# Loop work at other steps, and the single taps of two images' 3x3 convolution as 64-row matmuls on the two halves of the array

## What is computed

```python
om = conv3x3(x, w_om) + b_om                     # 64 -> 108 channels: o1, o2, mask
o1, o2, mask = split(om, 3)                      # 4 groups x 9 taps each
offset, mask = concat(o1, o2), sigmoid(mask)     # offset: (dy, dx) per tap and group
# for each tap k: v_k = bilinear sample of x at (position + tap k + (dy, dx)) * mask
out = relu(sum_k w_dcn[:, :, k] @ v_k)           # 64 -> 64 channels
```

## Time and the profile before

| | |
|---|---|
| time, median of 3 runs | 207.06 us (206.66 to 207.31) |
| the profiled execution's own time | 207.24 us |
| its span, first to last instruction | 205.1 us |
| busy: PE, DVE, ACT, POOL | 180.4, 161.3, 106.3, 86.2 us |
| mean granted TensorE clock | 0.998 of full speed |

### The profile page before, as it was taken

How to read it: one execution, slowest core, us unless ns; L and a number is a source line. 1 busy time by engine, 2 the same in 40 slices (tenths; PEclk the granted TensorE clock), 3 DMA queues, 4 the chain that set the end, 5 groups by cost and what they waited for, 6 DMA issues and landing times.

```text
span 205.1 us, 4582 instructions
## 1 busy us (share of the span) xinstructions
PE 180.4 (88%) x1806; PEld 127.2 (62%) x1806; DVE 161.3 (79%) x268; ACT 106.3 (52%) x199; POOL 86.2 (42%) x103
## 2 busy tenths in 40 slices
PE   0398997979899989999889999999969999998980
PEld 0234944644356544477578779639958789877870
DVE  0899778994768859887889779717999798899922
ACT  1146057500007784688748757836766687864000
POOL 8237952864013096504444344240661554442000
PEclk9999999999999999999999999999999999999999
DMA  6940000000130000010011000000002000000000
GB/s 189 327 33 2 3 0 0 3 0 0 29 77 19 20 27 9 25 36 3 9 36 25 0 3 0 3 0 3 9 25 70 20 2 16 0 16 2 19 0 21
DMA packets 8499, 5.54 MB, mean 27 GB/s; under 512 B 4887, under 2 KB 7461, under 8 KB 8473
## 3 DMA queue, kind: packets, MB, share of 16 engines
q1 hardware_dynamic: 8089, 4.25, 8.1%
q10 hardware_dynamic: 288, 0.89, 1.4%
q0 software_dynamic: 96, 0.06, 0.1%
HBM read 2.82 MB, written 0.52 MB: 16 GB/s over the span
## 4 chain that ended last, share of the span: by engine, by line
PE 66%; DVE 16%; ACT 6%; issue 4%; DMA 3%; POOL 2%; SPq 0%; DVEq 0%; ACTq 0%; POOLq 0%
PE ps L1254 20%; PE ps L1228 10%; PE ps L1148 10%; PE ps L1044 4%; PE ps L1165 3%; DVE smp_prod L777 3%; DMA x_parts<-in_x 3%; PE ps L1296 3%; PE ps L1302 3%; PE ps L1081 3%; PE ps L1213 2%; PE ps L1199 2%; DVE smp_prod L888 2%; PE ps L1182 2%; DVE windows_attention L873 1%
## 5 line engine op out<-in xcount | busy, mean ns | idle before, releaser
L888 DVE TENSOR_TENSOR smp_prod<-ps,hx_selx 128x768 f32<-128x768 f32 x72 | 67.5, 953 | 10.1 <-PE ps L1228 8.8
L1254 PE MATMUL ps<-smp_prod,windows_attention 128*64 128x192 f32 (+2 forms) x512 | 54.9, 336 | 0.0
L1254 PEld LDWEIGHTS ps<-smp_prod,windows_attention 128*64 128x64 f32 x512 | 40.1, 136 | 4.1 <-ACT windows_attention L575 0.3
L1228 PE MATMUL ps<-haty,by_rows 128*64 128x256 f16 x432 | 39.4, 275 | 2.0 <-DVE smp_prod L888 1.8
L451 POOL TENSOR_SCALAR disty<-disty 64x512 f32<-64x512 f32 (+1 forms) x23 | 13.5, 586 | 64.3 <-ACT haty L596 64.2
L1228 PEld LDWEIGHTS ps<-haty,by_rows 128*64 128x64 f16 x432 | 26.1, 109 | 9.7 <-DVE smp_prod L888 3.9
L604 ACT ACTIVATE hx_selx<-ps 128x512 f32<-128x512 f32 x36 | 21.3, 591 | 10.8 <-PE ps L1213 10.8
L458 POOL TENSOR_TENSOR haty<-disty,haty 64x512 f16<-64x512 f32 (+1 forms) x23 | 24.0, 1042 | 1.9
L1148 PE MATMUL ps<-conv_staged 128*108 128x512 f32 (+1 forms) x60 | 23.3, 521 | 0.7 <-ACT x_parts L568 0.7
L606 ACT ACTIVATE hx_selx<-hx_selx 128x512 f32<-128x512 f32 x36 | 22.7, 631 | 1.2
L591 ACT ACTIVATE disty<-ps 128x512 f32<-128x512 f32 (+1 forms) x24 | 12.5, 521 | 12.3 <-PE ps L1199 12.3
(11 more groups left out here) (140 smaller groups left out, 273.2 us busy)
## 6 DMA issues: line engine op xcount, KB each, us to landing
x_parts<-in_x SPq DMA_DIRECT2D x2, 256.0 KB, 5.2
bcast<-in_bcast SPq DMA_DIRECT2D x2, 256.0 KB, 6.6
x2seq<-x_parts SPq DMA_DIRECT2D x2, 256.0 KB, 3.7
out<-x_parts SPq DMA_DIRECT2D x8, 64.0 KB, 2.2
vals_attw<-in_cf ACTq DMA_DIRECT2D x1, 480.0 KB, 5.8
stack_m<-x_parts SPq DMA_DIRECT2D x12, 36.0 KB
kept<-in_cf ACTq DMA_DIRECT2D x1, 390.5 KB, 4.2
conv_staged<-in_wom SPq DMA_DIRECT2D x1, 324.0 KB, 6.8
```

What stands on the lines that cost most here:

```text
L888: nc.vector.tensor_tensor(pairs, rows, cols.unsqueeze(1).to_broadcast([P, QUARTERS, HW]), ALU.mult).then_inc(s_mult, 1)
L1228: ins = nc.tensor.matmul(ps[h * C:(h + 1) * C, at:at + HW], by_matrix(a, QUARTERS - 1 - k)[:, h * C:(h + 1) * C], haty[i % 2][:, p * HW:(p ...
L1254: return nc.tensor.matmul(dst[:, at:at + strips * 3 * SP].rearrange("p (s k n) -> p s k n", k=3, n=SP), rows, sampled(i, ki, m, first, str ...
```

## The change

Three tables of the loop are new, one more step constant moves, and the single taps are done in another way. The weights' upper half, zeros before, is filled by one POOL copy with the single taps' weights. A single tap is then a matmul on 64 rows only. Pieces 0 and 1 interleave theirs: those of piece 0 read partitions 0 to 63, those of piece 1 partitions 64 to 127, and they write different PSUM banks (4 and 0). In pieces 2 to 4 the single tap is a 64-row matmul between two 128-row ones.

```diff
-MASKS = [{4: (0, 0), 5: (0, 1), 6: (0, 2), 8: (0, 3)}, {0: (0, 4), 2: (0, 5), 6: (1, 0), 8: (1, 1)},
+MASKS = [{4: (0, 0), 5: (0, 1), 7: (0, 2)}, {0: (0, 3), 1: (0, 4), 3: (0, 5), 5: (1, 0), 7: (1, 1)},
...
-    (1, 2): (9, 6), (1, 3): (10, 6), (1, 4): (11, 4), (1, 5): (12, 4),
+    (1, 2): (9, 6), (1, 3): (10, 6), (1, 5): (11, 4), (2, 2): (12, 6), (2, 3): (13, 6), (2, 5): (14, 4),
+    (3, 2): (15, 6), (3, 3): (16, 6)}
...
-SEL_Y = {1: 0, 3: 1, 7: 2}
+SEL_Y = {2: 0, 6: 1, 8: 2}
-LATE = {0: (1, 1), 1: (2, 0), 2: (2, 1)}
+LATE = {0: (1, 1), 2: (2, 0), 3: (2, 1)}
...
+            pool.wait_ge(s_wom, 16)
+            singles = womt.rearrange("p (k s n) -> p k s n", k=3, s=2)[:, :, 1]
+            nc.gpsimd.tensor_copy(singles[C:P], singles[0:C]).then_inc(s_singles, 1)
+            pool.wait_ge(s_singles, 1)
...
-                    if m == 3 and i:
+                    if m == 4 and i:
                         values(i - 1, 2, it)
...
-                        if (i, m - 1) in PAIRS_AT:
-                            g, src = PAIRS_AT[i, m - 1]
-                            if g % 2:
+                        for at in (m - 1, m):
+                            g, src = PAIRS_AT.get((i, at), (0, 0))
+                            if g % 2 and (at == m) == (i > 0 and src == 4):
                                 window_out(g, it, src)
...
+            def conv_single(p, ky, upper, start, stop):
+                n, lo, hi = PIECES[p]
+                rows = slice(C, P) if upper else slice(0, C)
+                return nc.tensor.matmul(bank(CONV_BANK[p])[0:OM, lo:hi], womt[rows, (2 * ky + 1) * OM:(2 * ky + 2) * OM],
+                                        conv_source(PIECES[p], rows, 3 * ky + 2 - upper), start=start, stop=stop,
+                                        skip_group_check=True)
...
-            for p in range(2):
-                for k in range(TAPSTEPS):
-                    convolve(p, k)
+            pe.wait_ge(s_singles, 1)
+            pe.wait_ge(s_dup0, 1)
+            for ky in range(3):
+                conv_pair(0, ky, ky == 0, False)
+            pe.wait_ge(s_dup0, 2)
+            for ky in range(3):
+                ins = conv_single(0, ky, 0, False, ky == 2)
+                conv_single(1, ky, 1, ky == 0, False)
+            ins.then_inc(s_conv, 1)
+            for ky in range(3):
+                ins = conv_pair(1, ky, False, ky == 2)
+            ins.then_inc(s_conv, 1)
```

More of the change, by code:

```diff
@@ L280, in bass_local_attention_then_deformable_conv @@
         s_perm, s_wtap, s_wzero, s_wfin = sem("s_perm"), sem("s_wtap"), sem("s_wzero"), sem("s_wfin")
+        s_singles = sem("s_singles")
         s_stats, s_pair, s_eps, s_rstd = sem("s_stats"), sem("s_pair"), sem("s_eps"), sem("s_rstd")
@@ L1137, in _, with conv_source, conv_pair @@
             keep_warm(3)
+            def conv_source(piece, rows, tap):
+                n, lo, hi = piece
+                j = n % 2 * 2 + lo // HW
+                return shifted(dup[n // 2], tap)[rows, j:j + (hi - lo) // HW]
+            def conv_pair(p, ky, start, stop):
+                n, lo, hi = PIECES[p]
+                return nc.tensor.matmul(bank(CONV_BANK[p])[0:OM, lo:hi], womt[:, 2 * ky * OM:(2 * ky + 1) * OM],
+                                        conv_source(PIECES[p], slice(0, P), 3 * ky), start=start, stop=stop,
+                                        skip_group_check=True)
+            def conv_single(p, ky, upper, start, stop):
+                n, lo, hi = PIECES[p]
+                rows = slice(C, P) if upper else slice(0, C)
+                return nc.tensor.matmul(bank(CONV_BANK[p])[0:OM, lo:hi], womt[rows, (2 * ky + 1) * OM:(2 * ky + 2) * OM],
+                                        conv_source(PIECES[p], rows, 3 * ky + 2 - upper), start=start, stop=stop,
+                                        skip_group_check=True)
             def convolve(p, k):
-                n, lo, hi = PIECES[p]
-                h, j = n // 2, n % 2 * 2 + lo // HW
+                n = PIECES[p][0]
                 ky, single = divmod(k, 2)
                 if k == 0:
-                    if h == 0:
-                        pe.wait_ge(s_dup0, n % 2 * 2 + hi // HW)
+                    if n < 2:
+                        pe.wait_ge(s_dup0, J)
                     else:
                         pe.wait_ge(s_dup1, 2)
-                ins = nc.tensor.matmul(bank(CONV_BANK[p])[0:OM, lo:hi], womt[:, k * OM:(k + 1) * OM],
-                                       shifted(dup[h], 3 * ky + 2 * single)[:, j:j + (hi - lo) // HW], start=(k == 0),
-                                       stop=(k == TAPSTEPS - 1), skip_group_check=True)
+                if single:
+                    ins = conv_single(p, ky, 0, False, k == TAPSTEPS - 1)
+                else:
+                    ins = conv_pair(p, ky, k == 0, False)
                 if k == TAPSTEPS - 1:
@@ L1333, in sampling @@
                         if i < 3 and m == 6 and isinstance(it, int):
-                            windows_out(8 + 4 * i, it)
+                            windows_out(8 + 3 * i, it)
                         if i == 0 and m == 8 and isinstance(it, int):
@@ L1358, in sampling @@
                         g, dst = PAIRS_AT[i, m]
-                        if i == 0 or m in (3, 5):
+                        if i == 0 or m == 3:
                             windows_out(g - 1, it)
@@ L1366, in sampling @@
                     if m == FINAL and i:
-                        if i in (1, 2) and isinstance(it, int):
-                            windows_out(6 + 4 * i, it)
+                        if i in (1, 2, 3) and isinstance(it, int):
+                            windows_out(7 + 3 * i, it)
                         if i == FAR and isinstance(it, int):
@@ L1371, in sampling @@
                         final(i - 1, it)
-                for m in range(3):
+                for m in LATE:
                     block_of_products(B - 1, *LATE[m], it)
```

5 lines of the change are left out of this document (2 added, 3 removed).

## The result

| | before | changed kernel |
|---|---|---|
| time, median of the runs timed side by side | 207.34 us (206.66 to 207.48) | 205.53 us (204.86 to 205.99) |
| the profiled execution's own time | 207.24 us | 205.50 us |
| its span | 205.1 us | 203.6 us |
| mean granted TensorE clock | 0.998 | 0.997 |

The ratio is 0.9916, with a 95% interval of 0.9895 to 0.9937: the changed kernel is 0.6% to 1.1% faster. The forecast was 204.6 us with a range of 202.9 to 207.2; the time lies 0.9 us above the forecast.

What follows compares the result with a forecast made beforehand. The prediction took the loop as bound by PE with DVE close behind. Its terms, 0.0 - 1.5 - 1.5 - 0.2 + 0.45 = -2.75, rounded to -2.6, took the profiled 207.24 to 204.6 us, range 202.9 to 207.2.

Steps and rivals of the forecast that it cites:

- convolution ahead of the loop: Before the loop: first select_y 0.2 us earlier, two splits between the select_y's 0.22 later; net 0.0, ends -0.45 and +0.35.
- windows: In the loop: three PE waits for DVE's copies of window groups, 1.82 us together, mostly go; -1.5 us.
- bank 7 with the late block and its values: Loop: PE's stops for ACT's copy at PSUM bank 7 half won, -1.5 us; block and values one step later, -0.2.
- piece 4: Steps (3, 4) and (3, 5): alternating pairs and single taps make four new splits where PE is the bound, +0.45 us.
- POOL's copy: Copy of the single taps' weights on POOL: hidden in a 4.23 us gap, costs nothing; 0.5 us without that gap.
- the time of the interleaved passes: Sign in the convolution: the interleaved single taps' matmuls take about 1.5 us and not 2.6.
- the windows without a wait: Sign in the loop: no idle time of PE above 0.3 us before windows.
- the stretches: Signs between successive `final`s: 1 and 2 shorter by 1.2 to 1.8 us each, 3 about 1 longer, 5 and 6 0.3 to 0.7 shorter.
- The price of a split: PE going between matmuls on all and part of the array: 0.11 us each, from two convolution runs; a pass 0.437.
- the stops only move: Rival: PE, freed at bank 7, waits for DVE's multiplication instead; only -0.3 us in all, 206.9 us, chance 0.17.
- Row halves one after the other: Rival: the 12 interleaved single-tap passes don't run side by side, 2.62 us instead of 1.53; 205.5 us, chance 0.15.
- The late vertical weights: Rival: the spread in step 1 of images 1, 3, 5, 7 waits 0.85 us each for POOL; 208.0 us, chance 0.18.

Runs made afterwards that it cites:

- conv_only: Kernel before with only the convolution changed to the changed kernel's, 64-row single taps in all pieces; 208.49 us, ratio 1.0047.
- loop_only: Kernel before with the changed kernel's loop tables, values step and window-copy rule, convolution as before; 203.92 us, ratio 0.9821.
- bank7_and_late: Kernel before with the new masks, select_y steps, late block and values step; windows and convolution as before; 204.98 us, ratio 0.9869.
- own_weights: Changed kernel with the copied single-tap weights in their own buffer, so pieces 2 to 4 run single taps on 128 rows; 204.42 us, ratio 0.9839.
- singles_one_half: Changed kernel with piece 1's single taps also on partitions 0 to 63, behind those of piece 0; 205.99 us, ratio 0.9931.
- windows_only: Kernel before with only the windows' steps and the rule for their copies from the changed kernel; 207.48 us, ratio 0.9993.
- bank7_only: Kernel before with only the MASKS and SEL_Y tables of the changed kernel; 211.3 us, ratio 1.0192.
- late_only: Kernel before with only the blocks of steps 1 and 2 and the third values one step later; 207.23 us, ratio 0.9984.

## Why the prediction was right, and where its sizes were off

The sign and the range were right, and the main mechanisms in part. The sizes came out by some luck, as errors of both signs met in the sum. The terms, each beside what the runs showed:

| term of the prediction | predicted | measured | by |
|---|---|---|---|
| convolution ahead of the loop | 0.0 | +0.45 | start of conv_only against before, +0.43, and of the changed kernel against loop_only, +0.47 |
| windows | -1.5 | -0.65 | sums of loop_only and bank7_and_late |
| bank 7 with the late block and its values | -1.5 - 0.2 | -2.2 | sums of bank7_and_late and before |
| piece 4 | +0.45 | +0.7 | stretch 3, conv_only and own_weights |
| POOL's copy | 0 | 0 | start of the convolution, 59.40 in the changed kernel against 59.42 |

The measured terms add up to -1.7; the trace has -1.75. The table leaves out two small parts, the start of loop_only, 0.17 us earlier than before, and the last stretch, 0.05 longer, and it rounds the rest. The prediction's own sum was -2.75, rounded to -2.6.

Of the signs that it named, the time of the interleaved passes and the windows without a wait came. Of the stretches, only stretch 1 fell as said (1.54); 2 gained 0.91 where it said 1.2 to 1.8, 3 lost 1.87 where it said about 1, 6 gained 0.89 where it said 0.3 to 0.7, and 5 got longer. In stretch 3 the term for piece 4 was too small, and two groups of windows moved in: at 0.59 us each they alone are 1.2, so that with 0.45 for piece 4 the sum is 1.6.

**Ahead of the loop.** This term went wrong at "A DMA that took all of the 2.57 us would make the select_y 0.11 later, one that took 1.8 or less gives all of the 0.66. I take -0.2." The DMA takes nearly all of it. The chain of the changed kernel holds the pieces, from DVE's last part to the select_y:

```profile
64.50 0.44 DVE x_parts L862
64.94 0.43 SPq L368
65.38 0.04 issue
65.42 1.87 DMA stack_y<-x_parts
67.28 0.14 issue
67.42 0.30 PE ps L1226 x2
```

From the end of DVE's part to the select_y are 2.48 us, with no slack. If the transfer took as long before the change, the select_y was within 0.1 us of being bound by it then already (2.57 us from DVE's part), though the trace of before showed it right behind PE's own work. PE won 0.52 of the 0.66 us (it was free at 66.81, where it had started the select_y at 67.33), and this could only become a wait, of 0.61 with the 0.09 by which the select_y came later. The two splits had been counted as 0.22; they are 0.33. Both misses have one sign, 0.3 and 0.1 us.

**The price of a split.** This is the step that made piece 4 and the second select_y too cheap: "18x + s = 7.98 and 8x + s = 3.61 give x = 0.437 and s = 0.11". The two runs differ in more than their length, since the first one holds 24 passes of 256 columns, and s is the small remainder of two large numbers: 0.1 us more or less in them moves it by 0.08 or 0.18. The rows to take were two short runs of equal passes, and the chain of the kernel before has both, the 8 passes in 3.61 us of the earlier trace rows and

```profile
136.33 1.90 PE ps L1148 x4
```

They give 0.43 and 0.19, without an edit. With 0.18 piece 4 would have been +0.72 and measured +0.71. The interleaved passes were taken for seven slots; the pairs in own_weights make six, and with one entry, 6 x 0.215 + 0.18, that is the 1.48 us from 60.85 to the next pass on 128 rows at 62.33.

The Trainium skill ("TensorEngine Tiling (Array Packing)", Key Properties) says that a change of tiling mode drains the engine. The runs agree in kind, with 0.16 to 0.18 us a change, and between windows and tap, both on 128 rows and over 64 columns wide, there is no such price: the tap's two passes take 0.86 us in the kernel before, twice 0.43. The page "TensorE: Matmul & The Clock Gate" of the Trainium skill (Packing small matmuls) says in one sentence that weights load under running matmuls only where the row group differs. In another of the same section it also names loads into a background weight buffer. The runs speak against the first sentence alone: in singles_one_half all twelve passes are on one row group and take 2.77 us, 0.23 each, where passes with their loads in the open would need 0.22 and 0.17 more.

**Windows.** "The three waits sum to 1.82; I take -1.5" took waits for time. PE was to go on to the next spread, and that one waits for the multiplication of the step before on DVE. In windows_only this takes all of the gain. In the full set of tables 0.65 us are left; that DVE's work stands more evenly there is a likely reason, not a tested one. The rival "the stops only move" named exactly this wait, before the spreads, but priced it at bank 7; it held for the windows instead.

**Bank 7, block and values.** The term was -1.7 and the runs gave -2.2. The mechanism was right where it was named (the chain no longer goes through ACT in (5, 3)), but the size came in part from elsewhere: stretches 3 to 6, which had the stop and were to give 1.5, gave 1.02 in bank7_and_late (0.08, 0.26, -0.21 and 0.89), stretch 7 gave 0.60 where 0.2 was put down, and stretches 1 and 2 gave 0.57, which no term had. As a sum of two parts the term was wrong: priced one by one they are +4 and 0. The prediction had put the values' step down to evening out PE's work; bank7_only shows that it is what lets the masks move in image 1, and the waits in late_only suggest that the block's move needs the select_y of step 1 out of the way. That stretch 5 would be shorter by 0.3 to 0.7 was wrong: it is 0.21 or 0.22 longer, in every kernel in which both edits stand. By the tables it has one mask more than before, as has stretch 1, and stretches 4 and 6 have one less each (0.25 us each in the chain, so part of what 6 gained has only moved); I did not test this by itself.

**The rivals.** Row halves one after the other: refuted by 1.55 us for twelve passes. The late vertical weights: not seen, no spread in the loop waits for POOL. Stops that only move: true of the windows, and in small part of stretch 4, where PE's stop of 0.37 us for ACT went, one of 0.35 before a spread came, and the old one before a spread shrank from 1.19 to 0.86.

## What to carry to other kernels

A wait that ends an idle time is worth its length only if the next wait behind it has room: look at what the engine would meet after it. Here, with DVE busy for 89 and 82% of stretches 1 and 2, 0.65 us were left of 1.8. Edits of one schedule can need each other: price them together as well as one by one. Take the price of a change of shape from short runs of equal instructions in the trace, not from two long ones of mixed sizes. When an operand comes over a DMA, add up issue, transfer and the step behind it from the chain before counting time won on the engine that waits: here 2.48 us stood hidden under PE's own work. And where a kernel got slower by a long stop of PE, read the granted clock behind the stop before you put all of the loss down to the wait.

## What was not expected of the hardware

Two 64-row halves of the array, each with its own weights and its own PSUM bank, gave 12 f32 passes of 256 columns in 1.49 to 1.55 us where one half alone took 2.77: 1.8 times, with every load hidden. A 64-row tap between 128-row ones cost 0.16 to 0.18 us at each change, more than a third of a pass of 512 columns (0.43), and a 64-row pass itself took as long as a 128-row one. And in bank7_only the granted clock was 0.50 for 3.4 us after PE had stood still for 2.76, which made the stop about half as expensive again as its own length.
